# Rotating pairs of features by a scale and an addition instead of a matmul

## What is computed

```
L0: x = x + attention(LN(x)*(1+scale)+shift);  x = x + W2(gelu2(W1(LN(x)*g2+beta2)))
L1: h = gelu(x@down.T+down_b); h = expert_W[dom]@h + expert_b[dom] + domain_emb[dom]
    x = LN(h@up.T + up_b + x)*ln_gamma + ln_beta
L2: e = x.reshape(B, N, D//4, 4);  x0..x3 = e[..., 0..3]     # theta, phi: one each per batch
    out = stack([x0*ct + x1*st, -x0*st + x1*ct, x2*cp + x3*sp, -x2*sp + x3*cp], -1)
L3: as L1, with its own weights
```

## Time and profile before

| what | value |
|---|---|
| median of 3 runs | 1039.97 us (1037.59, 1039.97, 1044.8) |
| span of the profiled execution | 1036.6 us, 20438 instructions |
| PE, DVE, ACT, POOL busy | 92%, 78%, 71%, 70% of the span |
| mean granted TensorE clock | 0.986 |
| attention | 0 to 724 us |
| iterations 2 to 7 of the network | 775.4 to 984.5 us |
| end | 984.5 to 1036.6 us |

### The profile page before, as it was taken

How to read it: one execution, slowest core, us unless ns; L and a number is a source line. 1 busy time by engine, 2 the same in 40 slices (tenths; PEclk the granted TensorE clock), 3 DMA queues, 4 the chain that set the end, 5 groups by cost and what they waited for, 6 DMA issues and landing times. The chain is left out here.

```text
span 1036.6 us, 20438 instructions
## 1 busy us (share of the span) xinstructions
PE 956.1 (92%) x5892; PEld 640.9 (62%) x5892; DVE 813.7 (78%) x2075; ACT 734.7 (71%) x1211; POOL 726.3 (70%) x596
## 2 busy tenths in 40 slices
PE   5879999999999999999999999898999999999963
PEld 4646556656655655755665665454777777777752
DVE  8887797878879879879787887874456877887697
ACT  3577887888798788788788878875446556655433
POOL 3487697788788878878778878777555567755631
PEclk9989999999999999999999999999999999999987
DMA  7978978997996997897799799752111111111001
GB/s 262 334 289 292 381 289 278 363 347 238 346 384 214 336 386 257 291 390 292 265 372 343 237 348 370 252 193 82 41 41 41 42 33 50 42 41 41 21 21 41
DMA packets 127535, 230.33 MB, mean 222 GB/s; under 512 B 5488, under 2 KB 53872, under 8 KB 123632
## 3 DMA queue, kind: packets, MB, share of 16 engines
q1 hardware_dynamic: 127472, 229.60, 62.0%
HBM read 187.63 MB, written 41.94 MB: 221 GB/s over the span
## 5 line engine op out<-in xcount | busy, mean ns | idle before, releaser
L937 ACT ACTIVATE prob<-prob,nmax 128x512 f32<-128x512 f32 x512 | 357.0, 729 | 59.6 <-DVE nmax L762 56.4
L762 DVE CUSTOM_DVE_ANT_0 prob<-s_bank,big 128x512 f32<-128x512 f32 x512 | 338.7, 684 | 69.7 <-POOL big L1101 40.3
L1101 POOL TENSOR_TENSOR big<-big,mterm_early 128x2048 f32<-128x2048 f32 (+2 forms) x88 | 305.3, 3484 | 71.5 <-DMA big<-in_fside_Bx16xSxS 62.3
L593 PEld LDWEIGHTS t_bank<-ident,prob 128*128 128x128 f32 x2048 | 238.1, 141 | 168.3 <-issue 51.5
L593 PE MATMUL t_bank<-ident,prob 128*128 128x128 f32 x2048 | 317.7, 278 | 15.9 <-ACT prob L937 6.7
L944 ACT COPY pt<-t_bank 128x512 f32<-128x512 f32 x312 | 181.1, 584 | 51.7 <-PE t_bank L593 50.6
L581 PE MATMUL s_bank<-stack_k,stack_q 128*128 128x512 bf16 x512 | 195.4, 382 | 1.3 <-DVE nmax L762 0.7
L771 DVE COPY pt<-t_bank 128x512 f32<-128x512 f32 x200 | 137.2, 686 | 34.9 <-PE t_bank L593 34.6
L2052 POOL TENSOR_TENSOR gl<-big,gh 128x512 fp32r<-128x512 f32 x64 | 84.6, 1329 | 69.8 <-DVE gh L1643 69.8
L607 PE MATMUL o_bank<-pt,val 128*32 128x512 f32 x1024 | 122.9, 598 | 1.2 <-ACT pt L944 0.7
L1905 ACT ACTIVATE big<-bank,late 128x512 f32<-128x512 f32 x62 | 42.7, 689 | 75.2 <-PE bank L1446 71.4
(11 more groups left out here) (257 smaller groups left out, 1610.0 us busy)
## 6 DMA issues: line engine op xcount, KB each, us to landing
big<-in_fside_Bx16xSxS SPq DMA_DIRECT2D x128, 1024.0 KB, 8.0
pieces_dram<-pieces SPq DMA_DIRECT2D x64, 384.0 KB, 7.3
stack_q<-pieces_dram SPq DMA_DIRECT2D x15, 1024.0 KB, 8.3
stack_k<-pieces_dram SPq DMA_DIRECT2D x15, 1024.0 KB, 10.0
pieces_dram<-pieces SPq DMA_DIRECT2D x32, 256.0 KB, 7.6
xin<-in_x SPq DMA_DIRECT2D x8, 512.0 KB, 8.7
x_dram<-x SPq DMA_DIRECT2D x8, 512.0 KB, 2.6
x1r<-x_dram SPq DMA_DIRECT2D x8, 512.0 KB, 4.3
```

Source lines behind the costliest of these rows:

```text
L593: last = pe.transpose(t_bank[n % 2][:, c * P:(c + 1) * P], prob[:, n % NT, c * P:(c + 1) * P], ident[:])
L762: dve.tensor_tensor_reduce(out=prob[:, n % NT, :], in0=s_bank[n % 3][:, :], in1=bias[:, h % NB, t, :], scale=-1.0, scalar=3e38, op0=ALU.ad ...
L937: act.activation(tile, tile, ACT.Exp, bias=nmax[:, n % NT:n % NT + 1], scale=-1.0).then_inc(exped.sem, 1)
L1101: pool.tensor_tensor(bias[:, h % NB, tiles], bias[:, h % NB, tiles], mterm[:, tiles], ALU.add).then_inc(masked.sem, 1)
```

## The change

The features of L1's output are put even in half 0 and odd in half 1: TensorE transposes every second column of `xh`, and L3's weights, biases and L1's gamma and beta are laid out to match on the host. The last normalisation writes the features back in their own order. Then the partner of each feature is at the same place of the other bank. ScalarE's scale and shift carry cos and the whole offset, and VectorE adds sin times the other bank. The coefficients for all batches are made once, in iteration 1 at n = 9, by eight VectorE instructions of 128x8 (`turn_coefficients`). TURN_AT is 8, ROTATE_AT 9; `rotation_matrix` and its call at n = 2 go.

```diff
 to_features, TensorE
                 if i == 0:
-                    wait(pe, feat_done[1], j - 3, DC)
+                    wait(pe, x4_done, j - 3, DC)
                 for c in range(DC):
+                    at = slice(c * P, (c + 1) * P) if i == 0 else slice(c, D, DC)
                     for t in range(QT):
-                        last = pe.transpose(bank[2 + c][:, t * P:(t + 1) * P], xh[:, i, t, c * P:(c + 1) * P],
-                                            ident[:])
+                        last = pe.transpose(bank[2 + c][:, t * P:(t + 1) * P], xh[:, i, t, at], ident[:])
 TensorE, iteration
-                    if n == ROTATE_AT and on(j, 2):
-                        rotate(j - 2)
 VectorE
+            def turn_coefficients():
...
+            def take_turned(j):
+                wait(dve, feat_done[1], j, DC)
+                for c in range(DC):
+                    dve.scalar_tensor_tensor(x4[:, c], bank[3 - c][:, :], turn[:, 1, c, j:j + 1], feat[:, c], ALU.mult, ALU.add
+                                             ).then_inc(x4_done.sem, 1)
+            def turned_low(j):
                 for c in range(DC):
                     wait(dve, high_done[1], j, c + 1)
-                    dve.tensor_tensor(x24l[:, 1, c], bank[at + c][:, :], x24h[:, 1, c], ALU.subtract
+                    dve.tensor_tensor(x24l[:, 1, c], x4[:, c], x24h[:, 1, c], ALU.subtract
                                       ).then_inc(low_done[1].sem, 1)
-                for c in range(DC):
-                    dve.tensor_copy(x4[:, c], bank[at + c][:, :]).then_inc(x4_done.sem, 1)
-            def rotation_matrix(j):
...
+                    if n == TURN_AT and on(j, 2):
+                        take_turned(j - 2)
                     if n == ROTATE_AT and on(j, 2):
-                        take_rotated(j - 2)
+                        turned_low(j - 2)
 normalise, VectorE
-                    last = dve.tensor_scalar(xh[:, i, t], tile(i, t), mv[:, i, t, 0:1], rstd[:, i, t:t + 1],
-                                             ALU.subtract, ALU.mult)
+                    last = dve.tensor_scalar(features(xh[:, i, t], i), halves(tile(i, t)), mv[:, i, t, 0:1],
+                                             rstd[:, i, t:t + 1], ALU.subtract, ALU.mult)
 ScalarE
-            def rotated_high(j, at=4):
-                wait(act, rotated, j, 1)
+            def turned_high(j):
                 wait(act, down_done[1], j - 1, 1)
                 for c in range(DC):
-                    act.copy(x24h[:, 1, c], bank[at + c][:, :]).then_inc(high_done[1].sem, 1)
+                    wait(act, x4_done, j, c + 1)
+                    act.copy(x24h[:, 1, c], x4[:, c]).then_inc(high_done[1].sem, 1)
 rotation_input, ScalarE
-                    act.activation(feat[:, c], bank[2 + c][:, :], ACT.Identity, bias=k["beta_f"][:, c:c + 1],
-                                   scale=k["gamma_f"][:, c:c + 1]).then_inc(feat_done[1].sem, 1)
+                    act.activation(feat[:, c], bank[2 + c][:, :], ACT.Identity, bias=turn[:, 2, c, j:j + 1],
+                                   scale=turn[:, 0, c, j:j + 1]).then_inc(feat_done[1].sem, 1)
 the end, TensorE
-            rotate(y)
             last_features(0)
             last_features(1)
-            last_rotate(0)
             down(y, 1, at=2)
-            last_rotate(1)
             last_down(1, 0)
+            last_down(1, 1)
             expert(y, 1, at=2)
-            last_down(1, 1)
             up(y, 1, at=2)
 the end, VectorE
             normalise(y, 1)
-            rotation_matrix(y)
             last_take(0, 0)
             last_take(0, 1)
             last_statistics(0, 0)
             last_statistics(0, 1)
-            last_rotation()
+            take_turned(y)
             last_normalise(0, 0)
             last_normalise(0, 1)
-            take_rotated(y)
+            turned_low(y)
+            last_turned(0)
+            last_turned(1)
             last_low(1, 0)
+            last_low(1, 1)
             hidden_low(y, 1)
-            last_low(1, 1)
 the end, ScalarE
             last_rotated(0)
+            last_rotated(1)
             hidden(y, 1, at=2)
-            last_rotated(1)
```

More of the change, by code:

```diff
@@ L1331, in network_block @@
                 "norm"))
-        end_back, end_feats, end_rot, end_rotated, end_x4_done, end_out, end_stored, end_step = (
-            sem("end_" + n) for n in ("back", "feats", "rot", "rotated", "x4", "out", "stored", "step"))
+        end_back, end_feats, end_x4_done, end_out, end_stored, end_step = (
+            sem("end_" + n) for n in ("back", "feats", "x4", "out", "stored", "step"))
         END_A, END_B = (6, 7), (0, 1)
@@ L1411, in to_tokens @@
                     wait(pe, feat_done[0], j + 2, DC)
-                elif isinstance(j, int) and j == B - 2:
-                    wait(pe, x4_done, j, DC)
+                elif j == B - 2:
+                    wait(pe, norm_done[2], j - 1, 1)
                 else:
@@ L1504, in up @@
                 if l == 0:
-                    wait(pe, x4_done, j - 1, DC)
+                    wait(pe, norm_done[2], j - 2, 1)
                 elif at is None:
@@ L1593, in last_features @@
                         last = pe.transpose(bank[END_A[h]][:, c * EH + t * P:c * EH + (t + 1) * P],
-                                            end_xh[0][:, ET * h + t, c * P:(c + 1) * P], ident[:])
+                                            end_xh[0][:, ET * h + t, c:D:DC], ident[:])
                 last.then_inc(end_back, 1)
[L1597 to L1603, removed]
             to_tokens(y - 1, 2, x3[:, 1], x3_done[1])
@@ L1742, in iteration @@
                         low_part(j - 1)
-                    if n == 2 and on(j, 2):
-                        rotation_matrix(j - 2)
+                    if n == ROTATE_AT and j == 1:
+                        turn_coefficients()
                     for m, i in ((3, 1), (4, 2), (NORMALISE3_AT, 0)):
@@ L1780, in link, with last_turned @@
                 dve.wait_ge(end_step, steps[0])
-            def last_rotation():
-                link(dve.tensor_scalar(end_rotc[:], k["ident"][:], k["rot"][:, 0, z:z + 1], None, ALU.mult))
-                dve.scalar_tensor_tensor(end_rotm[:], k["beside"][:], k["rot"][:, 1, z:z + 1], end_rotc[:], ALU.mult, ALU.add
-                                         ).then_inc(end_rot, 1)
+            def last_turned(h):
+                dve.wait_ge(end_feats, DC * (h + 1))
+                for c in range(DC):
+                    dve.scalar_tensor_tensor(end_x4[:, c, cols(h)], bank[END_A[h]][:, (1 - c) * EH:(2 - c) * EH],
+                                             turn[:, 1, c, z:z + 1], end_feat[:, c, cols(h)], ALU.mult, ALU.add
+                                             ).then_inc(end_x4_done, 1)
             def last_low(l, h):
@@ L1828, in last_normalise @@
                 for t in range(ET):
-                    last = dve.tensor_scalar(end_xh[l][:, ET * h + t], bank[END_B[h]][:, t * D:(t + 1) * D],
+                    last = dve.tensor_scalar(features(end_xh[l][:, ET * h + t], 2 * l), halves(bank[END_B[h]][:, t * D:(t + 1) * D]),
                                              end_mv[:, l, ET * h + t, 0:1], end_rstd[:, l, ET * h + t:ET * h + t + 1],
@@ L1964, in iteration @@
                     if n == ROTATE_AT and on(j, 2):
[L1965 removed]
+                        turned_high(j - 2)
                     if n == INPUT_AT and on(j, -1):
@@ L2021, in normalise_before_last @@
                 for t in range(QT):
-                    last = act.activation(xh[:, 2, t], bank[4 + t // 2][:, (t % 2) * D:(t % 2 + 1) * D], ACT.Identity,
+                    last = act.activation(features(xh[:, 2, t], 2), halves(bank[4 + t // 2][:, (t % 2) * D:(t % 2 + 1) * D]), ACT.Identity,
                                           bias=std[:, 2, t:t + 1], scale=rstd[:, 2, t:t + 1])
@@ L2032, in _ @@
             rotation_input(y)
-            rotated_high(y)
+            turned_high(y)
             last_rotation_input(0)
```

78 lines of the change are left out of this document (36 added, 42 removed).

## The result

After the change the kernel takes 1048.32 us in the median of 9 runs (1043.94 to 1052.23). The kernel before, in 9 runs beside them, takes 1041.04 us (1037.59 to 1044.8). The ratio is 1.007, with a 95% interval of 1.0048 to 1.0092: some 7 us slower. The forecast was 1043.9 us with a range of 1035 to 1051.

What follows compares the result with a forecast made beforehand. TensorE's and VectorE's paths were taken to meet at the second to_features, with ScalarE the next limit. 2.3 + 0.9 - 2.5 - 1.0 = -0.3 us, plus 4.2 for the clock, on 1039.97: 1043.9 us, range 1035 to 1051.

Steps and rivals of the forecast that it cites:

- (a) to (c): Iterations 3 to 6: TensorE loses the rotation's 1.72 us, VectorE 1.7 us, of which ScalarE lets only 0.75 arrive.
- (c): Before normalise(j+1, 0): ScalarE's root is the next limit, so only 0.75 of VectorE's 1.7 us arrive.
- rival 2: TensorE is the bound, so removing L1477 wins 12.8 us in all: 1027.2 us, chance 0.07.
- (d): VectorE behind L1718: take_turned adds two instructions of 746 ns, 1.41 us together.
- (e): Second to_features: waits for take_turned to read banks 2 and 3, starts 0.58 us later; TensorE idles some 2.35 us.
- (g): ScalarE before network_input: turned_high is hidden, ending before L1430's result; without that cover up to 0.75 us.
- (h): VectorE before down: turned_low reads two SBUF tiles, but is hidden even with one POOL wait; two would use up the cover.
- rival 4: POOL holds up take_turned or turned_low: 5 x 1 us, 1045 without the clock's part, 1049 with it; chance 0.05.
- (j): Iteration 1: the coefficients' eight small VectorE instructions cost nothing, at most 1 us.
- rival 3: Strided read of xh slows the first L1430 of iterations 2 to 7; a doubling adds 5 us: 1049, chance 0.1.
- Rival 1: TensorE's gaps before the second to_features don't cost the clock: 1039.7 us, chance 0.3.

Runs made afterwards that it cites:

- b1: Kernel before, with the rotation's matmuls (L1477) cut from 512 to 2 columns in iterations 2 to 7 and for the last batch: 1041.09 us, ratio 0.9997.
- b2: Kernel before, with VectorE's rotation_matrix cut to 2 of 128 columns, TensorE's full rotation kept: 1037.12 us, a single run without a verdict.
- b3: Kernel before, with both the rotation's matmuls and VectorE's rotation_matrix cut to 2 columns: 1036.98 us, ratio 0.9968.
- e8: Kernel after, with 16 filling matmuls before the second to_features and POOL's output moved to n = 0 of the next iteration: 1039.98 us, ratio 0.9995.
- e4: Kernel after, with POOL's output moved from n = 8 to n = 0 of the next iteration: 1045.39 us, ratio 1.0037.
- e1: Kernel after, with take_turned put ahead of normalise(j+1, 0) on VectorE: 1044.29 us, ratio 1.0021.
- e3: Kernel after, with 16 unused matmuls filling TensorE's gap before the second to_features in iterations 2 to 6: 1044.62 us, ratio 1.0027.
- b4: Kernel before, with only the first to_features of each iteration reading every second column of xh: 1037.19 us, a single run without a verdict.
- e5: Kernel after, with take_turned ahead of normalise(j+1, 0) and POOL's output moved to n = 0 of the next iteration: 1039.59 us, ratio 0.9996.
- e7: Kernel after, with take_turned ahead of normalise(j+1, 0), POOL's output in the next iteration, normalise(j-3, 2) at n = 10: 1033.92 us, ratio 0.9935.

## Why the prediction was right or wrong

Right in kind: a small loss, 1048.32 us, inside the range of 1035 to 1051 and 0.3 us above its narrower one (1040 to 1048; by its own terms that upper end is 1047.1). The size of the loss is about half: 3.9 us were forecast over the kernel before, and 7.3 were measured between the medians, 6.8 in the profiled executions. One term was too dear, one was missing, and they partly cancel. By its own steps:

**(a) to (c), what is won.** TensorE's 1.72 us are worth nothing in iterations 3 to 6: b1 shows it, and with it that rival 2 (TensorE as the bound) is false, whatever suggests. Step (c) held in the kernel after: VectorE's L1719 starts 18.06 us into iteration 5, where L1713 started at 18.75, so 0.69 us of the 0.75 arrived, and ScalarE's root released it:

```profile
907.28 0.18 DVE L1719 RECIPROCAL rstd<-std 128x4 f32<-128x4 f32 x1 [0.20 <-ACT std L1936]
```

`take_turned` then spends them. What (c) had wrong is the slack behind the limit: VectorE was to be idle for some 0.9 us before the root, and it was for 0.1 to 0.2 (iterations 3 to 6). So b2 and b3, with the same instruction gone in the kernel before, get less than the 0.75 us: b2, where the rotation's matmul stays and at most 0.2 us was expected, nothing, and b3 0.75 us in every second iteration only, because POOL stalls the next instruction of VectorE instead. The prediction had not seen that.

**(d) and (e), the new wait.** The mechanism stands: the second `to_features` starts 21.6 us into the iteration against 20.9, released by `take_turned`, with 2.40 us idle ahead of it (2.35 forecast) and 742 ns an instruction (746 taken). The size of its price is the first mis-sized term. The start is 0.74 us later, not 0.58, but such a shift costs 0.28 us of iteration (e8), since TensorE before waited later on for `hidden_low`, held by POOL, and that slack takes up the rest. The prediction knew of 0.35 us of that slack and subtracted it from the clock's price, but not from the wait's: 2.3 us were taken for 1.1.

**(g) and (h), the halves.** (g) holds. (h) is the step that failed: "the pair ends at 902.7, or 903.8 with one such wait ... Hidden; with two waits of POOL's longer instructions that cover would be used up." It was two. The pair takes 4.34 us, behind both halves of POOL's `output`, which are 2.4 and 2.7 us long, and ends 25.9 us into the iteration, where TensorE was ready for `down` at 25.5. This costs 0.7 us in iterations 5 and 6 and 1.68 in 7 (after against e8 and e4): 3.1 us that the sum did not have. It had the price of the blocked case in its bounds, but took POOL's wait as a chance event of 0.05 for rival 4, where the order of the work makes it regular: `output` stands on POOL behind the last `gelu_low`, runs its two instructions back to back, and does so in each iteration just as VectorE comes to `turned_low`. In the kernel before it ran beside L1658, which reads PSUM and was not held (the row at 901.02 above). That row would have shown the place; it did not stand in the prediction.

The Trainium skill, "SBUF — State Buffer", section "SBUF: two separate sides", says that of a GpSimd instruction that reads SBUF and a VectorE instruction with two SBUF inputs the one that starts first holds the shared ports for its whole length, and the other is blocked. The trace agrees in both directions: `take_turned`, with one input in PSUM, took 743 ns at most, and `turned_low`, with two in SBUF, 2895. The change took a two-SBUF addition away (`rotation_matrix`) and, in the same stroke, moved a subtraction from PSUM's side to SBUF's.

**Iteration 2** is 1.07 us slower without the clock's part (e8, 34.87 against 33.80), forecast 0.9. **Iteration 7** gains 2.2 us without POOL's wait (33.26 against 35.47), forecast 2.5; with it only 0.53 was left. **The end** gains 0.92 us, forecast 1.0, and that is luck: TensorE runs low there for 13.7 us from 1008.0 and again from 1035.3 to the end, and in e1 and e3, whose end is the same code, it takes 50.43 and 50.55 us, next to nothing less than the 50.59 before. **The coefficients** (j) cost 0.1 us: iterations 0 and 1 take 48.71 us after and 48.64 before.

**The stride** costs little: 0.09 and 0.16 us in b4's iterations 2 and 7 and nothing in 3 to 6, and in the kernel after the first L1439 takes 1.11 us, under the 1.2 that would have spoken for rival 3. The other stride, in what the last normalisation writes, does not show either: L1724 has a median of 536 ns over all its instructions where L1718 had 530.

**The clock.** Three low stretches in five gaps, as forecast, at 1.5 to 1.6 us each, not 1.4. That the count came out is luck: e4, with the same gaps, had four, and the four gaps of 2.0 us had one each in e1 and e5. The medians of the mean clock, 0.977 against 0.983, say that the profiled execution is an ordinary one. Rival 1, no loss of clock, is what e3 made: 1044.62 us, not its 1039.7, because POOL's wait stays: e3's iterations 3 to 6 are 0.8 to 0.9 us longer than e8's, and iteration 7 is 1.7 us longer.

The sum, mended: +0.28 x 4 for the wait, 1.1; iteration 2, 1.07; iteration 7, -2.2; the end, -0.9; POOL, 0.7 x 2 + 1.68 = 3.1; the clock, 1.57 + 1.53 x 2 = 4.6. Together 6.8 us, and 6.8 were measured. (In iterations 3 and 4 POOL's wait lies under the low clock and is not counted. The terms are the table's differences, split by e8, so they must add up; what the experiments add is which part of each is whose.) The forecast had 3.9: 1.2 us too much for the wait, 3.1 missing for POOL, and some 0.4 too little for the clock. Another 1.1 us of the distance to 1048.32 is that the kernel before has a median of 1041.04 in the later runs and not 1039.97.

What stays open: why the clock falls after some of these gaps and not after others of the same length (the 2.40 us before 28.86 are followed by a clock of 1.00 in the execution before and by a low stretch at 28.4 us in those after, of e3 and of e7, where nothing is changed); and whether moving `normalise(j - 3, 2)` later would help the kernel before as well, where the rotation needs banks 4 and 5 at n = 9. That wasn't tried.

## What to carry to other kernels

An engine that is busy for 99% of an iteration need not bound it: find the instruction where two engines' paths meet, and ask of both what they win. Taking matmuls out of one side of such a meeting leaves an idle stretch, and that can cost more in clock than the matmuls were worth (here 4.6 us over three iterations, and the matmuls were worth nothing in iterations 3 to 6); fill it, or shorten the other side until it is gone. When an edit turns a VectorE operand from PSUM into SBUF, look up what GpSimd does at that very moment, instruction by instruction, and move its long pair away: here that took the ratio from 1.0027 to 0.9995 (e3 to e8). The time of a stalled instruction is not what its removal wins, since the stall can pass to the next one (b2, b3).

## What the runs showed of the hardware

**Stalls in series.** Two VectorE instructions of 0.68 us took 4.34 us beside two of GpSimd's: the second did not follow the first, but waited again, for GpSimd's next. Who is 0.01 us ahead decides: the cast takes 0.43 or 1.57 us, and GpSimd's instruction 1.57 or 1.30 (b3).

**Idle TensorE and its clock.** Gaps of about 2.4 us inside dense work were followed by a stretch of 3.4 us at 1.2 GHz in 3 of 5 cases (after) and 4 of 5 (e4), gaps of 2.0 us in 1 of 4 (e1) and 1 of 4 (e5), gaps of 1.1 to 1.5 us in none of five (e7). Sixteen matmuls without a use, 2.07 us of work, kept the clock in ten of ten gaps (e3, e8) and won 1.6 us in iteration 2.

**Strided weight loads.** Transposes load the strided operand as weights. By line, of the kernel after and then of b4 (ns min/median/max):

```profile
L1439 PEld LDWEIGHTS bank<-ident,xh x72: 137/196/212, 828.5 to 975.6; 128*128 128x128 f32 x72
```

```profile
L1431 PEld LDWEIGHTS bank<-ident,xh x72: 138/196/219, 821.6 to 963.8; 128*128 128x128 f32 x72
```

The 72 loads are of both kinds. Those of every second fp32 column take 194 to 219 ns, the contiguous ones 137 to 143 but for one of 163. The same line of the kernel before, all loads contiguous, has:

```profile
L1430 PEld LDWEIGHTS bank<-ident,xh x72: 137/140/143, 823.1 to 965.1; 128*128 128x128 f32 x72
```

It shows in a group of eight (1.09 us before, 1.23 in b4, 1.11 in the kernel after; why the two differ is open) and hardly in the iteration. The Trainium skill, "SBUF — State Buffer", section "Door 1: The DMA port swizzle", says that SBUF's lines have 16 bytes and that two hits in each are enough for full bandwidth; every second fp32 has two. For these weight loads the trace differs, by 40% and more, and the measurement decides.
